# Router normalisation and logits inside the second cross attention of a two-layer decoder

## The reference

```python
x = _layernorm(x + _L1_xattn_ref(x, ctx_1024, ctx_1024, mask, ...))   # cross attention over 64 keys, 16 heads
x = _layernorm(x + _L1_ffn_ref(x, ...))

def _L1_ffn_ref(x, ln_gamma, ln_beta, router_w, gate_up_w, down_w):
    xn = (x - mu) * rsqrt(var + 1e-5) * ln_gamma + ln_beta
    xf = xn.reshape(-1, D)
    logits = clip(xf @ router_w.T, -1e4, 1e4)          # 8 experts
    e = exp(logits - max(logits)); probs = clip(e / (sum(e) + 1e-8), 1e-8, 1.0)
    topk_p, topk_i = top_k(probs, 2)
    dense_gate = zeros(N, 8).at[arange(N)[:, None], topk_i].add(topk_p)
    for eid in range(8):
        xe = xf * dense_gate[:, eid:eid + 1]
        gate, up = split(xe @ gate_up_w[eid].T, 2)
        out = out + (silu(gate) * up) @ down_w[eid].T
    return x + out.reshape(B, S, D)
```

## Time and profile before

| | us |
|---|---|
| median of 3 runs (lowest, highest) | 1362.62 (1361.65, 1364.32) |
| the profiled execution | 1365.14 |
| its span | 1363.4 |
| busy in the span: PE, DVE, ACT, POOL | 1176.5, 871.6, 789.9, 599.9 |
| mean granted TensorE clock, share of full | 0.935 |
| second cross attention, from, to | 973.2, 1074.8 |
| experts up to the first gather | 1075.9, 1134.0 |
| expert loop and final norm | 1134.0, 1363.4 |

### The profile page before, as it was taken

The page is one execution under the profiler, slowest core; times in us unless marked ns, Lnnn a source line. Parts: engine busy times, 40 slices in busy tenths (PEclk is TensorE's granted clock), DMA queues, the critical chain, the costliest instruction groups (busy, mean ns, idle before and its releaser), DMA issues. The chain is left out here.

```text
span 1363.4 us, 25768 instructions
## 1 busy us (share of the span) xinstructions
PE 1176.5 (86%) x8215; PEld 872.0 (64%) x8216; DVE 871.6 (64%) x1536; ACT 789.9 (58%) x2129; POOL 599.9 (44%) x618
## 2 busy tenths in 40 slices
PE   7888589677799999999989999999799356999991
PEld 3544367455566777777666677767577254888881
DVE  2488789874245555566345556666588687888883
ACT  2488547423556655566455556665266355777773
POOL 1155437646454421530353232210166524888873
PEclk9999889887699999999999999999999756999996
DMA  9100000000110000000110000100460221333334
GB/s 300 44 1 1 0 1 1 1 16 16 28 36 17 16 17 16 17 17 1 32 32 16 17 1 17 47 1 2 163 209 1 74 92 55 53 54 55 55 50 135
DMA packets 42138, 58.29 MB, mean 43 GB/s; under 512 B 6608, under 2 KB 34640, under 8 KB 42032
## 3 DMA queue, kind: packets, MB, share of 16 engines
q1 hardware_dynamic: 34544, 46.70, 11.4%
q0 software_dynamic: 7488, 10.23, 4.7%
HBM read 32.80 MB, written 13.63 MB: 34 GB/s over the span
## 5 line engine op out<-in xcount | busy, mean ns | idle before, releaser
L2021 DVE TENSOR_REDUCE ga_neg_top<-ps 128x1 f32<-128x128 f32 (+7 forms) x256 | 182.0, 752 | 194.5 <-PE ps L1791 194.1
L1911 ACT COPY ga_e_tr<-ps 128x512 f32<-128x512 f32 (+3 forms) x192 | 92.1, 479 | 174.6 <-PE ps L1800 171.9
L1902 ACT ACTIVATE ga_e<-ps,ga_neg_top 128x128 f32<-128x128 f32 (+7 forms) x256 | 188.2, 743 | 7.5 <-DVE ga_neg_top L2021 6.8
L1800 PE MATMUL ps<-ident,ga_e 128*128 128x128 f32 x1152 | 165.1, 279 | 0.8 <-DVE ga_e_tr L2029 0.8
L1816 PE MATMUL ps<-ga_e_tr,ga_v 128*64 128x256 f32 x1152 | 151.7, 391 | 4.1 <-ACT ga_att L1919 4.1
L1800 PEld LDWEIGHTS ps<-ident,ga_e 128*128 128x128 f32 x1152 | 123.3, 142 | 28.0 <-ACT ga_e L1902 14.7
L2029 DVE COPY ga_e_tr<-ps 128x128 f32<-128x128 f32 (+3 forms) x192 | 105.8, 551 | 35.1 <-PE ps L1800 34.8
L2613 DVE TENSOR_TENSOR ex_w_lo<-ex_gate_up,ex_w_hi 128x1024 fp32r<-128x1024 f32 x78 | 95.5, 1225 | 35.1 <-ACT ex_w_hi L2467 32.1
L1976 POOL TENSOR_TENSOR ga_q_lo<-shared,ga_q_hi 128x1024 fp32r<-128x1024 f32 x15 | 35.5, 2369 | 174.7 <-ACT ga_q_hi L1892 174.7
L1816 PEld LDWEIGHTS ps<-ga_e_tr,ga_v 128*64 128x64 f32 x1152 | 72.4, 136 | 49.0 <-issue 23.4
L822 POOL TENSOR_TENSOR xa_e<-xa_e,xa_recip 128x1024 f32<-128x1024 f32 x32 | 60.9, 1902 | 68.7 <-DVE xa_recip L942 68.7
(11 more groups left out here) (335 smaller groups left out, 2830.8 us busy)
## 6 DMA issues: line engine op xcount, KB each, us to landing
shared<-shared SPq DMA_DIRECT2D x80, 128.0 KB, 2.4
ex_gate_up<-in_ex_gate_up SPq DMA_DIRECT2D x1, 8192.0 KB, 24.2
ex_down<-in_ex_down SPq DMA_DIRECT2D x1, 4096.0 KB, 35.8
x_tr<-in_x_tr SPq DMA_DIRECT2D x4, 512.0 KB, 7.0
x_nat<-in_x SPq DMA_DIRECT2D x1, 2048.0 KB, 11.4
gated_rows<-shared SPq DMA_DIRECT2D x8, 256.0 KB, 2.2
gated_rows<-x_tr SPq DMA_DIRECT2D x8, 256.0 KB, 2.3
x_tr<-summed_rows SPq DMA_DIRECT2D x8, 256.0 KB, 5.3
```

Source lines behind the costliest of these rows:

```text
L1800: last = nc.tensor.transpose(ps_tr[n % 2][:, (kb - k0) * P:(kb - k0 + 1) * P], e[half][t % 2][:, kb * P:(kb + 1) * P], core.ident[:])
L1902: nc.scalar.activation(e[half][t % 2][:, 0:blocks(t) * P], ps_scores(t, half), ACT.Exp, bias=neg_top[t % 2][:, half:half + 1], accum_out=s ...
L1911: nc.scalar.copy(e_tr[g % 2][:, k0:k1, half, t % 2 * P:(t % 2 + 1) * P], ps_tr[n % 2][:, 0:(k1 - k0) * P].rearrange("p (k t) -> p k t", t= ...
L2021: nc.vector.tensor_reduce(neg_top[t % 2][:, half:half + 1], ps_scores(t, half), AX.X, ALU.max, negate=True).then_inc(top_ready, 1)
```

## The change

A new class `Router` takes part in the second cross attention. The norm of a norm is folded: from the moments of z POOL makes two rstd and two offsets (one operation more, the others two columns wide). ACT writes each tile twice, into `x_nat` as before and, scaled by the second rstd, into `ro_scaled`; one step later PE turns that (in PSUM, the free half of `ps_ct`), ACT moves it to `x_tr` with gamma as scale and beta as bias, and in the step after PE makes the tile's logits. The stage has 23 steps in place of 21. SP loads router, gamma and beta ahead of the expert weights.

The experts' stage begins with the slot chain. Rows with tokens on the partitions are made by PE, which turns `x_tr` back (`turn_back`, 4 tiles at a time, in two places of its program); ACT weighs them straight out of PSUM in the order `WEIGHED`; the second copy goes over `doubled`, after that is in DRAM. SP stores 8 pieces of 512 KB, not 16 of 256 KB. `split_high` of experts 0 to 3 comes after the weighing, of 4 to 7 in the first two loop steps. `split_low` has 2 experts between chain and loop and 3 in each of the first two steps.

```diff
--- before.py
+++ after.py
+class Router:
+    LAGS = 7
+    def __init__(self, core, ctx):
+        self.core, self.dram = core, core.dram
+        self.gamma, self.beta = (core.sb(ctx, f"ro_{n}", [P, KD]) for n in ("gamma", "beta"))
+        self.router = core.sb(ctx, "ro_router", [P, KD, EXPERTS])
+        self.scaled = [core.sb(ctx, f"ro_scaled{i}", [P, D]) for i in range(2)]
+        self.xn_tr = core.x_tr
+        self.logits = core.ps_ct[:, D:D + TILES * EXPERTS]
+        self.ps_xn = core.ps_ct[:, 0:D]
...
+    def tiles_of(self, step):
+        return [step - lag if 0 <= step - lag < TILES else None for lag in (5, 6, 7)]
+    def load(self, sp):
+        sp.dma_start(self.router[:], self.dram["ex_router"].rearrange("(k p) e -> p k e", p=P)).then_inc(self.loaded, 16)
+        sp.dma_start(self.gamma[:], self.dram["ex_gamma_row"][0, :].rearrange("(k p) -> p k", p=P), allow_slow_non_contiguous=True).then_inc(self.loaded, 16)
+        sp.dma_start(self.beta[:], self.dram["ex_beta_row"][0, :].rearrange("(k p) -> p k", p=P), allow_slow_non_contiguous=True).then_inc(self.loaded, 16)
+    def pe_step(self, pe, step):
+        nc = self.core.nc
+        u5, u6, u7 = self.tiles_of(step)
+        if u7 is not None:
+            pe.wait_ge(self.moved, u7 + 1)
+            if u7 == 0:
+                pe.wait_ge(self.loaded, 16 * self.LOADS)
+            for k in range(KD):
+                last = nc.tensor.matmul(self.logits[:, u7 * EXPERTS:(u7 + 1) * EXPERTS], self.xn_tr[:, k, u7 * P:(u7 + 1) * P],
+                                        self.router[:, k, :], start=(k == 0), stop=(k == KD - 1))
+            last.then_inc(self.routed, 1)
+        if u6 is not None:
+            pe.wait_ge(self.scaled_ready, u6 + 1)
+            need(pe, self.moved, u6)
+            for k in range(KD):
+                last = nc.tensor.transpose(self.ps_xn[:, k * P:(k + 1) * P], self.scaled[u6 % 2][:, k * P:(k + 1) * P], self.core.ident[:])
+            last.then_inc(self.turned, 1)
+    def act_scale(self, act, u, z, offset, rstd):
+        need(act, self.turned, u - 1)
+        return self.core.nc.scalar.activation(self.scaled[u % 2][:], z, ACT.Identity, bias=offset, scale=rstd).then_inc(self.scaled_ready, 1)
+    def act_step(self, act, step):
+        nc = self.core.nc
+        u5, u6, u7 = self.tiles_of(step)
+        if u6 is not None:
+            if u6 == 0:
+                act.wait_ge(self.loaded, 16 * self.LOADS)
+            act.wait_ge(self.turned, u6 + 1)
+            for k in range(KD):
+                last = nc.scalar.activation(self.xn_tr[:, k, u6 * P:(u6 + 1) * P], self.ps_xn[:, k * P:(k + 1) * P], ACT.Identity,
+                                            bias=self.beta[:, k:k + 1], scale=self.gamma[:, k:k + 1])
+            last.then_inc(self.moved, 1)
...
-            nc.gpsimd.tensor_scalar(var_eps[:], mv[:, 1:2], LN_EPS, None, ALU.add).then_inc(eps_added, 1)
+            if router is not None:
+                nc.gpsimd.tensor_scalar(var_eps[:, 1:2], mv[:, 1:2], 1.0 + LN_EPS, LN_EPS * LN_EPS, ALU.mult, ALU.add)
+            nc.gpsimd.tensor_scalar(var_eps[:, 0:1], mv[:, 1:2], LN_EPS, None, ALU.add).then_inc(eps_added, 1)
             pool.wait_ge(eps_added, u5 + 1)
-            nc.gpsimd.tensor_tensor(rstd[:], var_eps[:], core.neg_half[:], ALU.pow).then_inc(rstd_ready, 1)
+            nc.gpsimd.tensor_tensor(rstd[:], var_eps[:], core.neg_half[:].to_broadcast([P, NORMS]), ALU.pow).then_inc(rstd_ready, 1)
             pool.wait_ge(rstd_ready, u5 + 1)
-            nc.gpsimd.tensor_scalar(offset[:], mv[:, 0:1], rstd[:, 0:1], -1.0, ALU.mult, ALU.mult).then_inc(offset_ready, 1)
+            nc.gpsimd.tensor_scalar(offset[:], rstd[:], mv[:, 0:1], -1.0, ALU.mult, ALU.mult).then_inc(offset_ready, 1)
...
             last.then_inc(q_ready, 1)
+        if router is not None:
+            router.pe_step(pe, step)
         if u4 is not None:
             pe.wait_ge(mixed_ready, u4 + 1)
...
             act.wait_ge(offset_ready, u5 + 1)
+            if router is not None:
+                router.act_scale(act, u5, z[:], offset[:, 1:2], rstd[:, 1:2])
             nc.scalar.activation(x_nat[:, u5, :], z[:], ACT.Identity, bias=offset[:, 0:1],
                                  scale=rstd[:, 0:1]).then_inc(xn_ready, 1)
+        if router is not None:
+            router.act_step(act, step)
...
-    BATCHED = BANK // D
+    BANKED = 2 * (BANK // D)
+    WEIGHED = [(0, 0), (1, 0), (0, 1), (1, 1)] + [(n, i) for n in range(2, TILES // BANKED) for i in range(2)]
...
-        KEPT = EXPERTS // 2
+        KEPT, AHEAD = EXPERTS // 2, EXPERTS // 4
...
-        ps_xn = [core.ps[:, i * BANK:(i + 1) * BANK] for i in (0, 1)]
+        ps_xn = [core.ps_s, core.ps_e]
...
-        gated = [scratch, xn]
+        def gated(i, t, count):
+            if i == 0:
+                return scratch[:, t:t + count, :]
+            return doubled[t // (TILES // 2)][:, t % (TILES // 2):t % (TILES // 2) + count, :]
...
-                for i in range(2):
-                    for g in range(GROUPS_OF_TILES):
-                        tiles = slice(g * GROUP, (g + 1) * GROUP)
-                        sp.wait_ge(gated_ready, i * GROUPS_OF_TILES + g + 1)
-                        sp.dma_start(gated_rows[i * N:(i + 1) * N, :].rearrange("(n p) d -> p n d", p=P)[:, tiles, :],
-                                     gated[i][:, tiles, :]).then_inc(gated_written, 16)
+                for turn, (n, i) in enumerate(WEIGHED):
+                    tiles = slice(n * BANKED, (n + 1) * BANKED)
+                    sp.wait_ge(gated_ready, turn + 1)
+                    sp.dma_start(gated_rows[i * N:(i + 1) * N, :].rearrange("(n p) d -> p n d", p=P)[:, tiles, :],
+                                 gated(i, n * BANKED, BANKED)).then_inc(gated_written, 16)
...
-                pool.wait_ge(dve_step, 3)
...
-                    pool.wait_ge(scaled_ready, g + 1)
-                    nc.gpsimd.tensor_tensor(xn[:, tiles, :], scratch[:, tiles, :],
-                                            beta_row[:].unsqueeze(1).to_broadcast([P, GROUP, D]), ALU.add).then_inc(xn_ready, 1)
...
-                pool.wait_ge(gated_written, 16 * 2 * GROUPS_OF_TILES)
+                pool.wait_ge(gated_written, 16 * 2 * TILES // BANKED)
...
+                def turn_back(n):
+                    if n >= 2:
+                        pe.wait_ge(gated_ready, WEIGHED.index((n - 2, 1)) + 1)
+                    for i in range(BANKED):
+                        for k in range(KD):
+                            columns = slice((n * BANKED + i) * P, (n * BANKED + i + 1) * P)
+                            last = nc.tensor.transpose(ps_xn[n % 2][:, (i * KD + k) * P:(i * KD + k + 1) * P], core.x_tr[:, k, columns], core.ident[:])
+                    last.then_inc(xn_ready, 1)
+                turn_back(0)
+                turn_back(1)
...
+                turn_back(2)
+                turn_back(3)
...
+                act.wait_ge(shifted_ready, 1)
+                nc.scalar.activation(probs[:], logits[:], ACT.Exp).then_inc(exp_ready, 1)
...
+                for n, i in WEIGHED:
+                    if n == 0:
+                        act.wait_ge(gates_ready, i + 1)
+                    if n == 0 and i == 1:
+                        act.wait_ge(summed_written, 16 * (TILES // DOUBLED + 1))
+                    if i == 0:
+                        act.wait_ge(xn_ready, n + 1)
+                    for j in range(BANKED):
+                        t = n * BANKED + j
+                        last = nc.scalar.activation(gated(i, t, 1).rearrange("p a d -> p (a d)"), ps_xn[n % 2][:, j * D:(j + 1) * D],
+                                                    ACT.Copy, scale=gates[:, i, t:t + 1])
+                    last.then_inc(gated_ready, 1)
+                for x in range(KEPT):
                     split_high(x)
+                act.wait_ge(gated_written, 16 * 2 * TILES // BANKED)
                 act.wait_ge(sources_ready, 1)
...
+                    if at(t, 0) or at(t, 1):
+                        first = KEPT + t * (EXPERTS - KEPT) // 2
+                        for x in range(first, first + (EXPERTS - KEPT) // 2):
+                            split_high(x)
...
+                for x in range(AHEAD):
+                    split_low(dve, x, down_first_ready)
...
-                        first = KEPT + t * (EXPERTS - KEPT) // 2
-                        for x in range(first, first + (EXPERTS - KEPT) // 2):
+                        first = AHEAD + t * (EXPERTS - AHEAD) // 2
+                        for x in range(first, first + (EXPERTS - AHEAD) // 2):
```

More of the change, by code:

```diff
@@ L971, in _ @@
             def _(pool):
-                for step in range(CROSS_STEPS):
+                for step in range(steps):
                     cross.pool_step(pool, step)
```

106 lines of the change are left out of this document (21 added, 85 removed).

## The result

The changed kernel takes **1347.44 us** (median of four runs, 1344.03 to 1349.18), the kernel before 1363.47 beside it: a ratio of 0.988 with a 95% interval of 0.986 to 0.991. The forecast was 1343.6 with a range of 1335 to 1351.5, so the sign and the size hold and the median lies 3.8 us above the number. The profiled execution took 1349.18 against the 1365.14 before: -16.0, where the sum said -19.0.

The account below looks back on a forecast made before the run. PE was taken to bound full steps; the path was norm and logits, chain, gather, loop. -34.3 + 6.6 + 2.8 + 2.0 + 1.5 + 2.4 = -19.0 gave 1346.1 profiled, 1343.6 us median, range 1335 to 1351.5.

Parts of the forecast that it names:

- Removed, -34.3: Experts' stage: the slot chain can be first, without norm and logits ahead of it; 34.3 us less.
- Full steps, +6.6: Second cross attention, PE-bound: logits and two transposes add 0.7 us per step, +6.6 us in all.
- all high ends: Total with every term at its upper end: -3.7 us; for full steps this took 10 x 0.74 more, +13.6.
- Drain, +2.8: End of the cross attention: ACT and POOL work ahead of PE's mix and unfitted router work, +2.8 us (1 to 5).
- two more steps, +2.0: After the cross attention's last offset: write, turn, moves, logits and hand-overs take 2.6, +2.0 us (1.4 to 3).
- The rival: PE's clock falls in the cross attention's steps, waiting for ACT; all ten full steps at half clock give 1405; chance 0.03.
- Weighed rows late, +1.5: Experts' stage before the first gather: weighed rows land at T+24, after the indices at T+22.3; +1.5 us (0 to 5).
- Loop start, +2.4: First two loop steps: DVE's third low half delays what is handed to PE, 2 x 1.2 = +2.4 us (0 to 4).

Follow-up runs that it names:

- kernel put together: Changed kernel plus unread PE transposes in the drain, router moves reordered on ACT, four low halves ahead of the loop, one semaphore per doubled-rows write: 1339.76 us.
- run with 24: 24 unread PE transposes between slot choice and first rows, six high halves ahead of the loop instead of four, against the kernel put together: 1337.55 us.
- run with own semaphores: Changed kernel with one semaphore for each write of doubled rows, so a weighing waits only for the write whose buffer it takes over: 1348.46 us.
- busy drain: Changed kernel with 8, 16 and 16 extra unread transposes at the end of PE's steps 16, 17 and 20: 1345.43 us.
- half of the logits: Changed kernel with one of the two parts of each tile's logits product left out, so its routing differs: 1342.50 us.

## Why the prediction was right, and where it was not

- **Removed, -34.3**: right. The chain's first operation is DVE's first, and its length did not change.
- **Full steps, +6.6**: +5.7. PE-bound at full clock, a step +0.62 where 0.7 was said. By the starts of PE's rows in one step (1056.22, 1056.59, 1056.84) the four logit passes take 0.37 and the two transposes 0.25; two passes fewer save 0.22. The sum's upper end is wrong: 10 x 0.74 more gives +14.0, not +13.6, and all high ends -3.3.
- **Drain, +2.8, and two more steps, +2.0**: this is the step that failed, together +11.4. Its parts on ACT and POOL are there, but all of it was priced at full clock, and the clock fell. With PE kept busy and the clock at 1.00 the same orders take +6.3 (27.98). So of the 6.6 us that the forecast lacks, 5.1 go with the clock, and 1.5 are the parts themselves, sized too small. The rival named the mechanism and put it into the full steps, where PE is full; its case against the drain was "the clock stays at 1.00 even through the drain, with PE 55% busy". That row was of a kernel whose longest wait there is 1.82, and two terms of the same sum, ACT's 1.2 to 1.4 and POOL's 0.7 ahead of the copy that PE waits for, lengthen just that wait. So the rival had the wrong place, and with it the wrong price (61 us) and the wrong chance (0.03): it happened in each of the seven traces that leave the stage as the change has it or only move its router work on ACT, and cost 3 to 5 us. A step that the sum makes later has to be carried into PE's gaps before the clock of the old gaps is used.
- **Weighed rows late, +1.5**: +2.4, with the right one waiting for the right other, but by other limits. (The term's own working, T+24.0 against T+22.3, gives 1.7; its 1.8 of latency has no row. The last row's landing came 4.55 us after its issue.) 1.9 of the 2.4 are POOL's later release, and 0.5 its copy of the indices, stretched by DVE's low half. The sum had these halves as free ("fit before the rows arrive"); they are what the first gather waits for in the end. In the kernel put together the rows let POOL go at 22.78, almost as early as the indices did before (22.60), and the gather still came at 24.98 and not at 23.72.
- **Loop start, +2.4**: +0.5 on the whole loop. The third half does stand in the chain, in the first step for 1.2, but PE at half clock, the table load and the SiLU on ACT hide part, and the starts of both kernels differ in their clocks too. Taking the third halves away gave 1.4. The low end, "0, if PE at half clock is later anyway", was the nearer one.
- The loop's pace, the last writes and the order of releases were as said. 1.4 us of the difference between the profiled executions lies ahead of the change, and is no effect of it.

So the total came out near the number partly by luck. For the profiled execution the sum is 3.1 too low, made up of +6.6 in the end stretch and +0.9 in the rows, against -1.9 in the loop start, -0.9 in the full steps and -1.4 and -0.2 that lie outside the change.

## What to carry to other kernels

When a change adds work between two engines in a stage where PE has gaps, write down PE's longest wait there before and after, not only its busy share: here 1.0 us more in two waits cost 3.6 us more in the products behind them, in a kernel whose only addition was three copies that nobody reads. Where such a gap can't be closed, products that nobody reads can fill it: 32 of them, in three steps, gave 3.8 us of end stretch. And take no price from totals alone when the stage holds such a step: leaving out 2.0 us of products showed as 5. And where DVE works beside a small operation of POOL that is on the path, look at how long that operation takes: here 0.18 us became up to 1.26.

## What was not expected of the hardware

- Waits of 2.02, 2.69 and 2.79 us on PE in the drain were each followed by the granted clock at 0.50. After one of 1.58 it fell too and was back within some 5 us; after 1.35, and after 1.82 in the kernel before, it did not fall. So the length of one wait does not decide it alone.
- Plain fp32 transposes against the identity raised the clock from 0.50 to 1.00 (1104 to 1108 in the run with 24).
- POOL's copy of 128x1 indices took 0.18 us with DVE idle and 0.46 to 1.26 us beside DVE's low halves (1.22 us each), always until about 0.05 us after the end of one.
- The rest of the row writes. In the run with own semaphores 1.9 us passed from the last full-rate moment to POOL's release (1113.5 to 1115.40), with a DMA share of 0.07, about one engine of 16, until 1114.8; in the kernel put together POOL was released after 0.7 us. The traces part in one thing: the seven in which the last row landed 24.0 to 24.5 us after the chain's start have a 16 KB packet of the page's kind `instruction` 18.7 to 21.0 us after it. The five with 22.7 to 23.5 have none there (four have it at 9.8 to 10.2, one not at all). That the packet holds the last row up was not tried.
- Two executions (the busy drain, and half of the logits) took 208.3 and 208.5 us from first gather to last scatter, against 206.7, with the same clock in the loop. Most of that is the first gather, which came 1.2 us earlier in both: from the chain's start to the last scatter they took 233.3 and 233.4, against 232.9. Why an earlier gather did not bring the last scatter forward is open.
